# A gated scan and a GRU on one core: the third chunk of x in scaled 16-bit halves, with two of the first-stage weight matrices split in one turn

## The reference, cut to what matters

```python
# layer 0, for all 64 x 128 positions at once, then sums along time
f = sigmoid(x @ W_f.T + b_f); i = sigmoid(x @ W_i.T + b_i)
f_n = f / (f + i + EPS); i_n = i / (f + i + EPS)
L = cumsum(log(f_n + EPS), axis=time)
hidden = cumsum(exp(L[last] - L[previous]) * i_n * (x @ W_h.T + b_h)) + exp(L) * cond
x = x + hidden
# layer 1, a recurrence of 128 steps over a state h of 64 x 512
z = sigmoid(x_t @ W_z + h @ U_z + vz); r = sigmoid(x_t @ W_r + h @ U_r + vr)
hh = tanh(x_t @ W + (r * h) @ U + vh)
h = (1 - z) * h + z * hh
x = x + h
```

## Time and profile before

| | us |
|---|---|
| time before, median of 3 runs | 1515.9 |
| lowest and highest of the 3 | 1515.52, 1516.64 |
| span of the profiled execution | 1513.4 |
| TensorE busy in that span | 1503.4 (99%) |
| VectorE busy | 1332.9 (88%) |
| ScalarE busy | 1066.1 (70%) |

### The profile page before, as it was taken

How to read it: one execution, slowest core, us unless ns; L and a number is a source line. 1 busy time by engine, 2 the same in 40 slices (tenths; PEclk the granted TensorE clock), 3 DMA queues, 4 the chain that set the end, 5 groups by cost and what they waited for, 6 DMA issues and landing times.

```text
span 1513.4 us, 58048 instructions
## 1 busy us (share of the span) xinstructions
PE 1503.4 (99%) x24698; PEld 1177.8 (78%) x24698; DVE 1332.9 (88%) x2928; ACT 1066.1 (70%) x2481; POOL 309.1 (20%) x333
## 2 busy tenths in 40 slices
PE   9999999999999999999999999999999999999998
PEld 7874444444444467779999999999999999999998
DVE  7999999999999889888888888888888888877787
ACT  7989999999999833656666666566666666656333
POOL 1100112111110014322222222222222222222222
PEclk9999999999999999999999999999999999999999
DMA  5156465565649978533333333333333333320000
GB/s 198 35 158 189 94 194 139 136 157 145 176 89 143 148 112 82 74 51 23 49 21 49 48 21 49 45 24 49 21 48 47 20 48 30 39 41 4 31 32 31
DMA packets 544979, 116.86 MB, mean 77 GB/s; under 512 B 520144, under 2 KB 527056, under 8 KB 536016
## 3 DMA queue, kind: packets, MB, share of 16 engines
q1 hardware_dynamic: 537424, 82.21, 31.2%
q0 software_dynamic: 7008, 30.41, 10.9%
q10 hardware_dynamic: 288, 0.52, 0.1%
HBM read 66.47 MB, written 33.55 MB: 66 GB/s over the span
## 4 chain that ended last, share of the span: by engine, by line
PE 97%; DVE 2%; issue 1%; ACT 1%; DMA 0%; DVEq 0%
PE ps L1458 33%; PE ps L1560 22%; PE ps L1523 22%; PE ps L1572 12%; PE ps L1544 5%; PE ps L1476 2%; DVE ST L1303 0%; PE ps L1425 0%; DMA AR<-in_w1f 0%; PE ps L1489 0%; DVE RL L1338 0%; DVE AR L1270 0%; DVE HL L1382 0%; DVE ST L1308 0%; DVE ST L1389 0%
## 5 line engine op out<-in xcount | busy, mean ns | idle before, releaser
L1458 PE MATMUL ps<-XH,WH 128*128 128x512 f16 x1872 | 404.7, 379 | 0.0
L1458 PEld LDWEIGHTS ps<-XH,WH 128*128 128x128 f16 x1872 | 182.9, 98 | 220.2 <-issue 0.3
L1560 PE MATMUL ps<-HL,U 128*128 128x64 f16 x8016 | 275.5, 193 | 2.0 <-DVE HL L1382 1.7
L1560 PEld LDWEIGHTS ps<-HL,U 128*128 128x128 f16 x8016 | 259.2, 98 | 8.5 <-issue 3.5
L1675 POOL TENSOR_TENSOR ST<-ST 128x256 f32<-128x256 f32 x127 | 107.9, 849 | 460.5 <-ACT ST L869 460.5
L847 ACT ACTIVATE ST<-ST 128x128 f32<-128x128 f32 x254 | 71.9, 310 | 169.5 <-DVE ST L1303 169.5
L1572 PE MATMUL ps<-HL,U 128*128 128x64 f16 x4064 | 163.2, 194 | 0.0
L1303 DVE SCALAR_TENSOR_TENSOR ST<-ps,dn,AR 128x128 f32<-128x128 f32 (+1 forms) x320 | 108.6, 372 | 46.8 <-PE ps L1572 44.2
L1303 DVE SCALAR_TENSOR_TENSOR ST<-ps,dn,XP 128x128 f32<-128x128 f32 x315 | 107.4, 372 | 41.2 <-PE ps L1572 38.9
L1572 PEld LDWEIGHTS ps<-HL,U 128*128 128x128 f16 x4064 | 138.6, 98 | 0.1
L1560 PEld LDWEIGHTS ps<-RL,U 128*128 128x128 f16 x3952 | 131.9, 98 | 6.0 <-issue 0.9
(11 more groups left out here) (201 smaller groups left out, 2976.4 us busy)
## 6 DMA issues: line engine op xcount, KB each, us to landing
x_scratch<-AR SPq DMA_DIRECT2D x16, 1024.0 KB, 5.3
AR<-in_x POOLq DMA_DIRECT2D x15, 1024.0 KB, 8.1
AR<-HB POOLq DMA_DIRECT2D x11, 1024.0 KB, 7.0
raw<-x_scratch SPq DMA_DIRECT2D x88, 128.0 KB, 4.5
out_y<-raw SPq DMA_DIRECT2D x11, 1024.0 KB, 4.6
raw<-in_x SPq DMA_DIRECT2D x10, 1024.0 KB, 7.4
ST<-in_x SPq DMA_DIRECT2D x5, 1024.0 KB, 7.3
out_y<-AR SPq DMA_DIRECT2D x4, 1024.0 KB, 4.3
```

The source lines that it names most:

```text
L1458: op = pe.matmul(ps[b][:, :], v[:, g, wp, k, e * P:(e + 1) * P], y[:, xp, k, :], start=n == 0, stop=n == 11)
L1560: pe.matmul(ps[b][:, col:col + B], U[:, g, uh, k, e * P:(e + 1) * P], S[:, k, 0], start=opens, stop=False, skip_group_check=True)
```

## The change

`WIDE` becomes 2, so chunk 2 is computed from 16-bit halves. The places of `XS` are exchanged (chunk c in place (c + 1) % 2), since `XH` lies over the second place and chunk 2's halves now go there while chunk 1 is still being multiplied. `w1x_hi` of W_f joins that of W_h in turn 1, and that of W_i goes to turn 2; `w1x_lo` of W_h and W_f are both in turn 2, and that of W_i in turn 3. Chunk 2's scale is made in VectorE's turn 2 (one more `exponent`). The later schedule is held where it was by constants (`SPLITS` = 6, `c < 5`).

```diff
--- before.py
+++ after.py
@@ -25,7 +25,8 @@
 EXPONENT = 0x7F800000
 FLOOR = 2.0 ** -90
 FLOOR1 = 2.0 ** -40
-WIDE = 3
+WIDE = 2
+SPLITS = 6
 EARLY = NCH - 2
 LOOK = 4
 LAST_LOOK = 9
@@ -127,6 +128,7 @@
         STAGE = {W1F: 0, W1I: 1, WR: 0, WZ: 1, WH: 0, UZ: 1, UR: 0, UH: 1}
         SPLIT = (WR, WZ, WH, UZ, UR, UH)
         W1_SPLIT = (W1H, W1F, W1I)
+        W1_TURNS = {1: (0, 1), 2: (2,)}
 
         X1, W1S, REST, XS0 = 6, 7, 10, 11
 
@@ -183,15 +185,15 @@
 
         def split_turn(q):
 
-            r, s = divmod(q - 2 * WIDE, 4)
+            r, s = divmod(q - SPLITS, 4)
             return (r, s) if 0 <= r < 6 else (None, None)
 
         def scaled_turn(q):
 
             r, s = split_turn(q)
             c = (q + 3) // 2
-            return ([W1S + 2, W1S] if q == 1 else [W1S + 1] if q == 2 else []) + ([r] if s == 1 else []) \
-                + ([XS0 + c] if q % 2 and WIDE <= c < NCH else []) + ([X1] if q == NQ - 4 else []) \
+            return ([W1S + 2, W1S] if q == 1 else [W1S + 1, XS0 + WIDE] if q == 2 else []) + ([r] if s == 1 else []) \
+                + ([XS0 + c] if q % 2 and WIDE < c < NCH else []) + ([X1] if q == NQ - 4 else []) \
                 + ([CS0] if q == 7 else []) + ([CS0 + 1 + C_SCALE[q]] if q in C_SCALE else [])
 
         SCALED = [i for q in range(NQ) for i in scaled_turn(q)]
@@ -512,7 +514,7 @@
                 if q in (4, 5):
                     sp.wait_ge(s_w1xlo, q - 2)
                     load_stage(SPLIT[q - 4])
-                if q == 2 * WIDE:
+                if q == SPLITS:
 
                     sp.wait_ge(s_mm[2], 4 * WIDE)
                     for n in range(2):
@@ -596,7 +598,7 @@
             w1_hi(0)
             for k in range(KT):
                 act.wait_ge(d_x0[k], 16)
-                act.activation(XS[:, 0, 0, k], by_k(xbuf[0])[:, k], ACT.Copy).then_inc(s_x0hi, 1)
+                act.activation(XS[:, 1, 0, k], by_k(xbuf[0])[:, k], ACT.Copy).then_inc(s_x0hi, 1)
             for i in range(1, len(W1_PIECES)):
                 w1_hi(i)
 
@@ -605,7 +607,7 @@
                 if c >= 2:
                     act.wait_ge(s_mm[2], 4 * (c - 1))
                 if c < WIDE:
-                    act.activation(XS[:, c % 2, 0], by_k(xbuf[c % 3]), ACT.Copy).then_inc(s_xhi, 1)
+                    act.activation(XS[:, (c + 1) % 2, 0], by_k(xbuf[c % 3]), ACT.Copy).then_inc(s_xhi, 1)
                     return
                 act.wait_ge(s_up, scaled(XS0 + c))
                 act.activation(XH[c % 2][:, 0], by_k(xbuf[c % 3]), ACT.Copy, scale=up[:, scale(XS0 + c)]).then_inc(s_xhi, 1)
@@ -802,8 +804,8 @@
                 if q == 0:
                     w1_magnitudes(W1F)
                     w1_magnitudes(W1I)
-                if 1 <= q <= 3:
-                    w1x_hi(q - 1)
+                for i in W1_TURNS.get(q, ()):
+                    w1x_hi(i)
                 r, s = split_turn(q)
                 if s == 0:
                     magnitudes(r)
@@ -910,7 +912,7 @@
             w1_lo(0)
             for k in range(KT):
                 dve.wait_ge(s_x0hi, k + 1)
-                dve.tensor_tensor(XS[:, 0, 1, k], by_k(xbuf[0])[:, k], XF[:, 0, 0, k], ALU.subtract).then_inc(s_x0lo, 1)
+                dve.tensor_tensor(XS[:, 1, 1, k], by_k(xbuf[0])[:, k], XF[:, 1, 0, k], ALU.subtract).then_inc(s_x0lo, 1)
             for i in range(1, len(W1_PIECES)):
                 w1_lo(i)
 
@@ -984,7 +986,7 @@
                     dve.wait_ge(s_mask, 1)
                 if c not in DIRECT and h == 0:
 
-                    if c < WIDE + 2:
+                    if c < 5:
                         dve.wait_ge(s_mm[2], 4 * WIDE)
                     else:
                         dve.wait_ge(d_sum[c % 2], sums_added(c - 1 if (c - 1) % 2 == c % 2 else c - 2))
@@ -1011,7 +1013,7 @@
             def x_lo(c):
                 dve.wait_ge(s_xhi, c)
                 if c < WIDE:
-                    dve.tensor_tensor(XS[:, c % 2, 1], by_k(xbuf[c % 3]), XF[:, c % 2, 0], ALU.subtract).then_inc(s_xlo, 1)
+                    dve.tensor_tensor(XS[:, (c + 1) % 2, 1], by_k(xbuf[c % 3]), XF[:, (c + 1) % 2, 0], ALU.subtract).then_inc(s_xlo, 1)
                 else:
                     dve.scalar_tensor_tensor(out=XH[c % 2][:, 1], in0=by_k(xbuf[c % 3]), scalar=up[:, scale(XS0 + c)],
                                              in1=XH[c % 2][:, 0], op0=ALU.mult, op1=ALU.subtract).then_inc(s_xlo, 1)
@@ -1168,8 +1170,8 @@
                 candidate(2 * q)
                 if q == NQ - 1:
                     early_lo()
-                if 2 <= q <= 4:
-                    w1x_lo(q - 2)
+                for i in W1_TURNS.get(q - 1, ()):
+                    w1x_lo(i)
                 r, s = split_turn(q)
                 if s in (2, 3):
                     split_lo(r, s - 2)
@@ -1454,7 +1456,7 @@
                             pe.wait_ge(s_xhi, c)
                         if c and h == 0 and i == 0 and n == 2 * KT:
                             pe.wait_ge(s_xlo, c)
-                        v, y = (W, XS[:, c % 2]) if c < WIDE else (WH1, XH[c % 2])
+                        v, y = (W, XS[:, (c + 1) % 2]) if c < WIDE else (WH1, XH[c % 2])
                         op = pe.matmul(ps[b][:, :], v[:, g, wp, k, e * P:(e + 1) * P], y[:, xp, k, :], start=n == 0, stop=n == 11)
                     op.then_inc(s_mm[g], 1)
```

## The result

The changed kernel takes 1518.38 us (median of 13 runs, 1516.4 to 1520.0); the kernel before, run beside it, 1515.09 us (13 runs, 1513.59 to 1516.64). The ratio is 1.0021, 95% interval 1.0013 to 1.0029: 3.3 us slower, just over what a measurement can tell. The forecast of 1518.5 us stood 2.6 above the 1515.9 of the three runs shown. So the time was met to 0.1, the difference was 0.7 short, and the sum came out through errors that cancel, as the trace shows. That it was met to 0.1 is luck.

A forecast was written before the change was run, and what follows sets the result against it. TensorE, busy 99%, was taken to bound the kernel, with VectorE almost without room. A 4.6 us wait less the 1.55 gain made TensorE 3.05 late, 2.6 after give-back: 1515.9 + 2.6 = 1518.5, range 1517.1 to 1521.0.

The forecast's parts named there:

- Step 1: Chunk 2 on TensorE: 16-bit halves take 31.09 us instead of 32.64, a gain of 1.55 if no wait.
- Steps 2 and 3: ScalarE's extra split in turn 1 makes VectorE 1.22 late; VectorE's second split in turn 2 adds 2.26, making 3.48.
- The base: Starting time of the sum: median 1515.9, reached from the trace's span of 1513.4 by adding 2.5 us.
- Step 4: VectorE's turn 3 split of W_i ends at 81.86; TensorE, due at 77.38 in chunk 2, waits 4.6 us.
- The forecast's failing step: Forecast's own case, new wait in chunk 2 without a clock fall: 1518.5, spread 1518.0 to 1519.1, chance 0.52.
- The rival with it: Clock falls in chunk 2's new wait, costing about 2 us: 1520.4; chance 0.28.
- Step 5: End of chunk 2: TensorE reaches chunk 3 at 109.6 against 106.56, 3.05 us late.
- Step 6: First cond product at 216: TensorE's 0.67 wait partly gives lateness back; VectorE's `c_low` 2.58 late, TensorE leaves 2.6 late.
- The rival with no wait in chunk 2: VectorE reaches W_i's split by 75.0; TensorE 1.55 early, but `c_low` 1.22 + 0.1 late at 216: 1517.2; chance 0.10.
- The rival faster: Chunk 2's gain of 1.55 reaches the end: 1514.4; chance 0.05.

The follow-up runs named there:

- filled waits: Changed kernel with 17, then 12, matmuls of zeros put ahead of TensorE's wait for the low half of W_i: 1517.95 and 1517.34 us.
- gate i later: Changed kernel with TensorE's two groups of gate i fourth and fifth instead of second and fourth in chunk 2's first turn: 1515.54 us.
- other split turns: Changed kernel with gate i later and W_h split by ScalarE in turn 2 instead of turn 1: 1514.91 us; with cond products a turn later, 1513.56.
- the last version: Changed kernel with gate i later, other split turns, later cond products, and two cond matrices' largest magnitudes taken over a quarter of the columns: 1512.93 us.
- W_f on GpSimd: Changed kernel with gate i later and cond products later, and W_f's low half made by GpSimd instead of VectorE: 1518.06 us.
- the run with 3.36 us: Changed kernel with the cond products one turn later: 1518.66 us.

## Why the prediction was right or wrong

- **Step 1** held: 16-bit matmuls of chunk 2 come at 0.216 (16 in 3.63 us), no longer at 0.2267, and the 1.55 is in the sum up to chunk 3.
- **Steps 2 and 3** held in kind. (Two of the six operations of the new `exponent` take 0.23 and 0.28, not at most 0.15; they lie in VectorE's wait, so it costs nothing.) Every start came about 0.7 earlier than forecast, since the load of W_h arrived 0.73 earlier. That arrival differs between executions: VectorE's scan of turn 1 began at 46.53 in the profile of before that the forecast was worked from, and at 45.2 to 46.1 in the 13 others, at 45.40, 45.92 and 46.12 in the three whose kernel is that of before up to there. The forecast took one execution's phase as the rule.
- **The base** was 0.8 too high, for another reason: 1515.9 is the median of the first three of 13 runs whose median is 1515.1. In every run listed the time is 1.7 to 1.9 above the span, so the profiled execution of before, with its 1513.4, took about 1515.2, and 2.5 was too much to carry its sums to the median with.
- **Step 4**, the wait of 4.6, was right in place, releaser and count of matmuls, and too large: 3.86. The difference is the 0.7 of steps 2 and 3.
- **The forecast's failing step** is the case without a fall of the clock. The rival with it was the true one; it said about 2 us, and it was 1.67 in the profile, 1.45 to 1.52 by the filled waits, and 2.9 in one other profile. Its 1520.4 was 2.0 too high: 0.8 of base, 0.7 of wait, 0.3 of clock, and 0.2 unplaced.
- **Step 5**: 4.03 late for 3.05, that is -0.7 of wait and +1.7 of clock.
- **Step 6** held: the sigmoid 3.50 late (4.03 - 0.53), `c_low` and TensorE 3.55, 0.48 given back (0.45 forecast). With the cond products a turn later nothing is given back (5.47 at chunk 3, 5.46 at the second stage). Of the 5.0 for 3.3 in the times, though, up to 1.2 can be the longer low stretch.
- **The rival with no wait in chunk 2** was priced at 1.3 over before (1517.2). Made true by gate i later, it costs 0.6: TensorE is held by `c_low` as said, and `c_low` is 0.62 late instead of 1.32. VectorE starts 0.8 earlier in this profile too (45.75), which would fit, but TensorE starts 1.25 earlier as well, so which of them sets the 0.62 is not shown.
- **The rival faster** was rightly put down to VectorE: with gate i later and other split turns TensorE loses nothing in chunk 2, and still the time is that of before, until VectorE has less to do. What the prediction did not name is the second place where VectorE holds TensorE then, x's low halves (L1014, L1016), at 106, 169 and 201.

What stays open: what makes the pauses of the second stage, and why executions spread. Those of the changed kernel spread over 3.6 us, but those of the kernel before, which has no such wait, over 3.1 (1513.59 to 1516.64). What differs between profiles of programs with the same work is the start (chunk 2 at 72.67 to 74.55), the pauses (1.0 us in three places, at 805.9, 866 and 928, in the slowest execution of the last version), and, where TensorE had a long wait, the length of the low stretch (3.4 and 6.8 us). Of the changed kernel's 13 runs the slowest two have the lowest mean clocks (0.996 and 0.997), but the fastest two (0.998) are no higher than most. How the spread divides among the three is not shown.

## What to carry to other kernels

When a consumer is moved to an earlier place, work out when it wants each operand there, in its own order of groups, and set this beside the producer's queue: here the saving of 1.55 us bought a wait of 3.9, and gate i's groups moved back by one or two places in TensorE's order keep it away (the time is then that of before, not less). A wait of that length on TensorE is to be costed with a fall of the clock behind it, here 1.7 us more, and 2.9 in one run. Where a second engine is busy 98% of the time, its lateness is passed on at every later place where the first one waits for it, so a wait that is removed comes back at the next such place until that engine gets less work or later due times. And a sum worked from one profile carries that execution's chance with it: here 0.7 us in the arrival of one load, and 0.7 us in pauses.

## What was not expected of the hardware

- The clock fell around idle times of 3.69 us, 3.36 us and 2.46 us (W_f on GpSimd), and stayed low for 3.4 us, 6.8 us and 3.4 us, the longest not for the longest idle. In the changed kernel it fell 1.3 us after TensorE had gone on, in the run with 3.36 us while it was still idle. In the runs with 1.0 to 1.1 us idle it held. The prediction had only the fall after 4 us at the end. The Trainium skill (page "TensorE: Matmul & The Clock Gate", Part 1) calls the low level the default that activity releases; by that rule an idle TensorE may fall back, and the trace agrees, with the 3.69 us.
- Pauses within rows of matmuls that wait for nothing (0.26 to 0.94 us idle at 685 to 694 us, others up to 1468 us) differ between kernels with the same instructions on TensorE, and are as large as the effects that were sought (1.3 us in one run).
- While GpSimd was in an operation of 5.46 us, a 128x3 operation of VectorE took 4.81 us: work handed over to GpSimd was paid for by VectorE.
